# A Mamba scan on one core: the moments of the router beside it move one step earlier, and so do its reciprocal deviation and its normalised rows

## The reference

```python
def step(h, inp):                       # scan over time, per channel i and state s (16 states)
    dA_t, dBu_t, C_t = inp
    h = dA_t * h + dBu_t
    y_t = jnp.einsum('bis,bs->bi', h, C_t)
    return (h, y_t)
...
y = ys.transpose(1, 0, 2) + u * D_param
y = y * jax.nn.silu(z)
return y @ out_proj_w.T + residual
...
# the expert layer gets _layernorm(x)
m = jnp.mean(x, axis=axis, keepdims=True)
v = jnp.var(x, axis=axis, keepdims=True)
return (x - m) / jnp.sqrt(v + eps)
...
router_logits = x_flat @ gate_w
router_probs = jax.nn.softmax(router_logits, axis=-1)
expert_idx = jnp.argmax(router_probs, axis=-1)
```

## Time and profile before

| what | value |
|---|---|
| time, median of 3 runs | 1321.23 us (1320.41 to 1322.44) |
| profiled execution, its own time | 1321.65 us |
| its span on the core | 1319.8 us |
| busy TensorE / VectorE / ScalarE / GpSimd | 1068.4 / 929.4 / 882.2 / 542.2 us |
| mean granted TensorE clock | 0.922 of full speed |
| scans, 128 (line 930) | 290.6 us busy, 2280 ns each |
| products with C, 128 (line 680) | 300.7 us busy, 2368 ns each |

### The profile page before, as it was taken

One profiled execution on the slowest core, in us unless ns is written; L12 is line 12 of the kernel. 1 busy time (PEld: TensorE's weight loads), 2 busy tenths in 40 slices (PEclk: granted clock), 3 DMA queues, 4 the chain that ended last, 5 costly groups with the idle time before them and its releaser, 6 DMA issues. The chain is left out here.

```text
span 1319.8 us, 24580 instructions
## 1 busy us (share of the span) xinstructions
PE 1068.4 (81%) x7230; PEld 735.7 (56%) x7230; DVE 929.4 (70%) x2003; ACT 882.2 (67%) x1835; POOL 542.2 (41%) x367
## 2 busy tenths in 40 slices
PE   1776499879778878656984999998999999991797
PEld 1332277678677777535981454544454544541796
DVE  5999489889789788634661767776685767663464
ACT  1877599989899889514651757565574656660564
POOL 0466388898988988832440001010101010011244
PEclk9988599999999899887995999999999999996899
DMA  3000133223453354203322000000000000001331
GB/s 86 2 3 2 36 94 96 90 88 101 129 188 112 120 163 114 53 33 104 92 83 63 3 1 14 5 18 1 17 0 18 0 17 5 13 18 52 87 86 50
DMA packets 50629, 74.36 MB, mean 56 GB/s; under 512 B 7351, under 2 KB 28604, under 8 KB 50528
## 3 DMA queue, kind: packets, MB, share of 16 engines
q1 hardware_dynamic: 41504, 51.09, 13.6%
q0 software_dynamic: 5568, 12.66, 2.7%
q10 hardware_dynamic: 3456, 9.46, 2.3%
HBM read 57.86 MB, written 16.24 MB: 56 GB/s over the span
## 5 line engine op out<-in xcount | busy, mean ns | idle before, releaser
L930 DVE TENSOR_TENSOR_SCAN h<-d_a,p_dbu 128x1024 f32<-128x1024 f32 x128 | 290.6, 2280 | 59.1 <-ACT d_a L728 50.6
L680 POOL TENSOR_TENSOR h<-h,c_rep 128x1024 f32<-128x1024 f32 x128 | 300.7, 2368 | 42.3 <-DVE h L930 40.6
L1853 ACT ACTIVATE at_probs<-at_scores,at_min 128x512 f32<-128x512 f32 x256 | 184.0, 721 | 136.4 <-DVE at_min L1963 88.0
L1963 DVE CUSTOM_DVE_ANT_0 at_scores<-at_p_scores,arena 128x512 f32<-128x512 f32 x256 | 174.5, 685 | 91.2 <-PE at_p_scores L1729 53.1
L720 ACT ACTIVATE b_du_T<-arena,b_T 128x256 f32<-128x256 f32 x512 | 216.7, 495 | 0.1
L1211 POOL TENSOR_SCALAR r_row<-r_row 128x4 f32<-128x4 f32 x16 | 3.7, 230 | 475.8 <-DVEq L1124 475.8
L813 PE MATMUL p_dbu<-ident,b_du_T 128*128 128x128 f32 x1024 | 170.6, 298 | 25.2 <-ACT b_du_T L720 22.5
L728 ACT ACTIVATE d_a<-arena,a_exp 128x511 f32<-128x511 f32 x256 | 169.1, 709 | 0.0
L1736 PEld LDWEIGHTS at_p_probs_T<-ident,at_probs 128*128 128x128 f32 x1024 | 113.0, 142 | 93.2 <-issue 71.0
L1736 PE MATMUL at_p_probs_T<-ident,at_probs 128*128 128x128 f32 x1024 | 159.3, 284 | 6.2 <-ACT at_probs L1853 5.8
L1729 PE MATMUL at_p_scores<-arena,at_q_T 64*128 64x512 f32 x512 | 158.3, 647 | 5.3 <-DVE at_min L1963 3.7
(11 more groups left out here) (220 smaller groups left out, 1534.8 us busy)
## 6 DMA issues: line engine op xcount, KB each, us to landing
c_rep<-c_rows SPq DMA_DIRECT2D x128, 256.0 KB, 3.3
f_row<-expert_rows SPq DMA_DIRECT2D x78, 129.0 KB, 2.0
arena<-in_w_all ACTq DMA_DIRECT2D x8, 578.0 KB, 4.2
arena<-bias_by_distance ACTq DMA_DIRECT2D x8, 448.0 KB, 4.0
x_tok<-in_x SPq DMA_DIRECT2D x4, 512.0 KB, 5.4
x_tok<-x_between SPq DMA_DIRECT2D x8, 256.0 KB, 2.8
expert_rows<-f_pad SPq DMA_DIRECT2D x10, 129.0 KB, 3.0
expert_rows<-f_pad ACTq DMA_DIRECT2D x8, 129.0 KB, 3.0
```

The lines of the kernel that those rows point to most:

```text
L680: nc.gpsimd.tensor_tensor(h[:, n % HS, :, :], h[:, n % HS, :, :], cc, ALU.mult).then_inc(prod_done, 1)
L930: nc.vector.tensor_tensor_scan(h[:, n % HS, :, :].rearrange("p c t -> p (c t)"), da[:, s % 2, :, :].rearrange("p c t -> p (c t)"), p_dbu[: ...
L1853: nc.scalar.activation(pr[:, s % 2, :], sc[:, s % 2, :], ACT.Exp, scale=-1.0, bias=mn[:, s % 2:s % 2 + 1]).then_inc(probs_ready, 1)
L1963: V.tensor_tensor_reduce(sc[:, s % 2, :], psc[:, s % SCB, :], band[:, hd, w0:w0 + T], 1.0, 3.0e38, ALU.add, ALU.min, mn[:, s % 2:s % 2 + 1 ...
```

## The change

The moments of the router (VectorE stage 1, `bn_aggr`) go from step 9 to step 8, where they follow stage 0 directly. ScalarE's `act_rstd` and GpSimd's `pool_rows` go from step 11 to step 10. TensorE's turn (step 13) and ScalarE's copy of it (step 14) stay where they are. The instructions are the same, and so are their waits.

```diff
@@ -683,7 +683,7 @@
                 for s in range(NS):
                     if s == 7 and b > 1:
                         rt.pool_send(pool, b - 2)
-                    if s == 11 and b > 0:
+                    if s == 10 and b > 0:
                         rt.pool_rows(pool, b - 1)
                     times_c(b, s)
 
@@ -730,7 +730,7 @@
 
             def early(b, s, after_scale):
 
-                if s == 11 and after_scale:
+                if s == 10 and after_scale:
                     rt.act_rstd(act, b)
                 elif s == 14 and after_scale:
                     rt.act_turned(act, b)
@@ -951,7 +951,7 @@
-            EARLY = {0: 8, 1: 9, 4: 14, 5: 15}
+            EARLY = {0: 8, 1: 8, 4: 14, 5: 15}
             LATE = {6: 0, 7: 1, 8: 2, 9: 3, 10: 4, 11: 5}
```

## The result

| | before | after |
|---|---|---|
| time, median | 1321.28 us (1320.41 to 1322.44, 4 runs) | 1307.40 us (1304.96 to 1309.33, 4 runs) |
| profiled execution, its own time and span | 1321.65, 1319.8 us | 1307.45, 1305.6 us |
| mean granted TensorE clock | 0.922 | 0.932 |
| idle before the scans (VectorE, line 930) | 59.1 us | 43.0 us |
| idle before the products (GpSimd, line 680) | 42.3 us | 29.8 us |

The ratio of after to before is 0.9898, 95% interval 0.9882 to 0.9913: 13.5 us less (11.5 to 15.6) by the ratio, 13.9 by the medians. A second comparison on another chip gave 0.9900 (0.9884 to 0.9917), 13.2 us. The forecast was 1307.7 us.

What follows compares the result with a forecast made beforehand. GpSimd's queue up to ScalarE's copy, then ScalarE through the scans, set the 50.40 us period. 5 x 2.34 = 11.7, plus 1.8 for the clock, gave 13.5 us: 1321.2 - 13.5 = 1307.7 us, range 1304.8 to 1312.0.

Steps and rivals of the forecast that it cites:

- The ring: The 50.40 us period: c(6) to ScalarE's copy, 22.06 us, set by GpSimd's queue; copy to next c(6), 28.34, by ScalarE.
- the term of 2.34 us: GpSimd's rows no longer wait for one product, c(10), so they start 2.34 us earlier per batch.
- The rows' waits are over: At the rows' new place on GpSimd, deviation (328.9) and earlier sends (by 331) are ready before they start at 336.66.
- Moments and deviation: VectorE's moments at step 8, ScalarE's deviation at step 10: a new wait of 0.2 to 0.3 us, hidden before the copy.
- c(10) behind the rows: GpSimd's product c(10) ends at 342.11 instead of 339.00, delaying TensorE's sum; cost nothing, with a few tenths to spare.
- The turn at the upper clock: TensorE's turn takes 0.63 instead of 1.08 us in four batches, after about 1.3 us of idle: 1.8 us saved.
- Five batches: Only b2 to b6 gain, 5 x 2.34 = 11.7 us; b1 has no wait to lose, b7's 3.30 us is no gain.
- GpSimd caught up: Rival 3: GpSimd, its slack down from 3.58 to 1.24 us, doesn't catch up; 2.5 to 7.5 us lost, chance 0.12.
- Rows beside the scans: Rival 5: VectorE's scans shut GpSimd's moved rows out of SBUF; 9.5 us slower, 1330.7, chance 0.02.
- ScalarE became the bound: Rival 2: rows come even sooner and ScalarE's busy time limits, 1305.3; chance 0.05 together with b7's wait counting.
- Behind the scan: The stages behind the scan are shifted whole, so the saving reaches the end of the launch unchanged.
- signs of being wrong: Late rows, a period hanging on `sum_up` or late c(6), or a saving differing between b7's end and the launch's end.

## Why the prediction was right, point by point

- **The ring, and the term of 2.34 us.** Right. Three products before the rows, first part of the ring 19.25 us, second part unchanged. 5 x 2.34 + 1.8 = 13.5 was forecast; the five periods shrank by 13.48. The two terms are right one by one as well: from the send to the rows it is 2.29 to 2.35 us less in b2 to b6, 11.64 in all, and from the turn to the copy 0.46, 0.46, 0, 0.46 and 0.45 us less, 1.83 in all. b4, whose turn was at the upper clock before too, shows the first term by itself: its period fell from 49.93 to 47.64, 2.29 us.
- **The rows' waits are over.** Right. They start at the end of c(9) without a gap, and the run with the rows alone gives the same time, so they did not even need the other two moves.
- **Moments and deviation.** Right in both sizes: a new wait of 0.26 us before Ln (0.2 to 0.3 forecast), hidden by the wait before the copy. Worth nothing by themselves, within 0.02 us over five periods.
- **c(10) behind the rows.** Right that it costs nothing: TensorE waits 0.73 us, but comes to the `spread` of step 15 at 341.25, just before ScalarE ends the `scale` for it (339.66 + 1.70 = 341.36). I had seen that the sums of c(10) get a wait, and not that those of c(9) are what forbids the next step.
- **The turn at the upper clock.** Right: 0.63 us in all of b2 to b6, and the copy waits 0.42 us where 0.4 to 1.1 was given. The two runs with extra transposes put the turn's duration at 1.7 us. In the kernel before the turn took 1.08 to 1.09 us in four of five batches at a granted clock of 0.50. I had chosen the upper level because 1.3 us of idle lay nearer to the one row than to the other. That it held in every batch owes something to luck: with the rows at step 9 the clock fell after 2.0 us of idle in b3 and not in b4. TensorE: Matmul & The Clock Gate in the Trainium skill (Part 1, What's actually happening) says that the throttled clock is the default and that activity releases it. The runs with extra transposes agree: all ten turns at 0.65 or 0.66 us.
- **Five batches.** Right: moving the rows in b7 alone brings 0.
- **Rivals.** GpSimd caught up (0.97 us of gaps left, about 1 forecast). Rows beside the scans took 3.13 us, as before, so no scan shut them out. Here the evidence ahead of the result was weaker than I put it: in b1 the scan that began beside the rows covered 2.29 of their 3.15 us and not all, and in b3 of the kernel before the rows (339.00 to 342.13) already lay beside a scan for 1.7 us (it ran from 338.42 to 340.71), so not mostly in idle time. In the changed kernel scans lie beside 2.7 of the 3.13 us. SBUF — State Buffer in the Trainium skill (Who interferes with whom) says that a VectorE instruction with two SBUF inputs contends with a GpSimd instruction that reads SBUF; the scan has only one input in SBUF, and the trace agrees. ScalarE became the bound only one move later.
- **Behind the scan.** Here the agreement of the launch owes something to chance. I had shifted everything behind the scan whole. The stretch from the last product to the end of the stage took 37.45 us before (554.83 to 592.28) and 36.70 after (541.42 to 578.12), so the last product came 13.41 us earlier and the end of the profiled execution 14.20. Such a difference was one of the signs of being wrong that I had named. It lies behind the last product, where the ring no longer acts. Why the stretch is shorter is not shown: its mean granted clock was lower after (0.78) than before (0.81).

## What to carry to other kernels

When several engines work in written-out order, look for the ring that sets the period: which queue decides from A to B, and which from B to A. An item moved forward by one place in a queue that runs without gaps gains just one item per turn of the ring, until the next engine is full or until something that its consumer handles first falls behind it. Count the items on both sides of such a hand-over: here the lag of four steps between product and sum fixes the best place. And where launches scatter by several microseconds from stages that are not touched, measure the stretch that is. When it has moved, cut it into legs before naming a cause: two runs here held a cost or a gain that was not the one they were made to show.

## What the runs showed of the hardware

- The same idle time of TensorE, 3.72 to 3.75 us, was followed by turns at both levels of the clock within one execution (0.63 in b4, 1.08 in b3, rows 5), and the run with the rows moved in b7 alone showed one of 0.86 us in b3. With the rows at step 9 it was so after only 2.0 us: in b3 the sums and the turn behind it ran at a granted clock of 0.54, in b4 at 1.00. In b2 to b7 of the changed kernel, its second trace and the run with the rows alone, after 1.1 to 1.7 us of idle, and behind filling work, all turns took 0.63 to 0.66.
- Work of no use on TensorE, 24 to 28 transposes that stand in its idle time, shortened the scan by 2.2 us: 4 x 0.43 us by turns at the upper clock, and 0.1 us a batch by turns that started sooner after the rows (3.18 us against 3.28).
- GpSimd's four tensor_scalar took 3.12 to 3.15 us wherever they stood, with 1.7 us of them beside a scan of VectorE (b3 before) or 2.7 (b3 after).
